# Laying the layers' first projections into the list of the first attention's last batch

## The chip, the cores and the metric

The kernel runs on one core of a Trainium2 chip. The metric is the device time of one execution in microseconds; three executions of the kernel before gave 3595.04 to 3600.91 us, median 3598.8 us.

## The reference, cut to what matters

The input is 8 batches of 512 tokens with 128 features. A block of two parts is applied:

```python
# part 1, "attention": queries, keys of 16 heads x 16 features, values of 64
A = tril((1 + q.k/4 + (q.k)^2/32))          # taylor features of q and k, multiplied out
y = A @ v;  y = y * rsqrt(mean(y*y) + 1e-5) * g;  out = y @ Wo.T
...
# part 2, six layers: x = x + local_attention(x); x = x + feed_forward(x)
qkv = x @ Wqkv                               # 16 heads of 64; q, k scaled to length 1
q, k = rotary(q), rotary(k)                  # two tables and a swap of halves
attn = softmax(q.k * 8 over the own and the previous window of 32) ; x += (attn @ v) @ Wo
x += W2 @ (a * gelu(gate)),  (a, gate) = layernorm(x) @ W1
```

Around both parts stand layer norms over the 128 features ("in" ahead of the attention, "mid" behind it, "x" ahead of the layers, "end" behind them). So the layers of a batch need that batch's attention and two norms, but nothing of another batch.

## The kernel before, in words

All work is cut into stages, each with a short name and a key. The function `order()` makes one list of all stages; each engine's program walks this one list from front to back and issues its own part of every stage that it has a part in. So within an engine the order is the order of the list, and between engines only semaphores count. `order()` gives each stage a place, a number from the table PLACE plus a multiple for its batch, tick or slot, and sorts by it. Places have no direct meaning in time: they fix only who comes ahead of whom.

The attention has 8 batches with 24 ticks each; one tick is a place unit. AS (scores) writes banks 0 to 3 of PSUM in turn, ASa and ASd square and mask them, AY multiplies with the values into bank 4, AE copies the sum to AO, AEa squares it, AR sums the squares into bank 5. AI1 to AI3 form the root of the mean square (logarithm and exponential on ScalarE, then three Newton steps on VectorE and a split), AM spreads it over the partitions, AMd multiplies, AO (8 accumulated products) projects. Then the norms mid and x, each as N1 (product on TensorE, Square and Copy on ScalarE), N2 (mean on TensorE) and N3 (Ln and Exp on ScalarE, three steps on VectorE); between them AZ (a VectorE product and a GpSimd addition); at the end AW writes X, the layers' input. In the steady part the tail of batch b lies beside the ticks of batch b+1; behind batch 7 there is no next batch.

The layers have 384 slots, one for each of 6 layers, 8 batches and 8 pairs of heads; one slot is a place unit there. LW loads a chunk of the weights into one of three buffers WS (issued from ScalarE's queue, and the fourth waits until GpSimd is through with the first), WC rounds it into LH on ScalarE, WL writes the rest into LL on GpSimd. XS and XSl do the same with X. PJ (one for q and one for k of each slot) multiplies three times on TensorE; PQ squares on ScalarE; PT multiplies with the rotary tables on VectorE; TS swaps halves by DMA; AD adds on GpSimd; SS sums squares on TensorE into bank 4. For every four slots NM1, NM2 form the roots, RW writes them to DRAM, RQ turns them for the queries, and RB (one per slot) reads them back, spread over the partitions; PR multiplies K with them on GpSimd. S1 (one per two slots) is the first score product; it needs PR of both slots. MX, S3, SU, NP, TT, PX, PV follow. LO and L2 load the output and feed-forward weights.

What matters here: `order()` calls `run()` behind the attention, which empties its plan, and only then plans the layers. So every layer stage comes behind AW of batch 7 in every engine's queue, and LW 0, LO, L2 and XS wait for `xa_dve` 16 (all of X) besides. The layers' memory overlays the attention's: the inner `ExitStack` is closed ahead of LH. Three banks, 5 to 7, serve the layers' groups in a ring; the attention's own ring is 6 and 7.

Of the kernel before, what the change touches and what calls it, by code (L numbers as in the profile page):

```python
# [138 lines left out]
def order():  # L139
# [21 lines left out]
    def norm(kind, b, z, places):  # L161
# [40 lines left out]
    run()  # L202
    o.ring, o.busy = [5, 6, 7], {}

    def group(st, i, by, value):
        at = o.ring.pop(0)
        o.ring.append(at)
        o.hold(at, st, (i,), 0)  # L210
        o.busy[at] = (by, value)
        o.put(st, i)


    for l in range(DEPTH):
# [11 lines left out]
        at(first + 2, o.put, "L1", l)
        at(first + 4, group, "WB", l, "wb_dve", l + 1)
        at(first + 9, o.put, "W1", l)
        at(first + 9.9, o.put, "W1l", l)  # L230
        at(first + 5 if l else -9.5, o.put, "LO", l)
        at(first + 10 if l else -9.5, o.put, "L2", l)
    for u in range(NB * DEPTH):
        z = 8 * u
# [12 lines left out]
        at(z + P["F3l"], o.put, "F3l", u)
        for i in range(2):
            at(z + P["TB"][i], o.put, "TB", u, i)
        for i in range(3):  # L250
            at(z + P["F4"][i], group, "F4g", 3 * u + i, "f4_act", 3 * u + i + 1)
            at(z + P["F4"][i], group, "F4a", 3 * u + i, "f4_dve", 3 * u + i + 1)
        at(z + P["F5"], group, "F5", u, "f5_dve", 2 * u + 2)
    for n in range(NS):
        for w in range(2):
            i = 2 * n + w
            at(n + P["PJ"][w], group, "PJ", i, "pj_dve", i + 1)
            at(n + P["PQ"][w], o.put, "PQ", i)
            at(n + P["PT"][w], o.put, "PT", i)
            at(n + P["SS"], o.put, "SS", i)  # L260
            at(n + P["AD"], o.put, "AD", i)
        at(n + P["TS"], o.put, "TS", n)
        at(n + P["RB"], o.put, "RB", n)
        at(n + P["PR"], o.put, "PR", n)
        if n % 4 == 0:
            at(n + P["NM1"], o.put, "NM1", n // 4)
            at(n + P["NM2"], o.put, "NM2", n // 4)
            at(n + P["RW"], o.put, "RW", n // 4)
            at(n + P["RQ"], group, "RQ", n // 4, "rq_act", n // 4 + 1)
        if n % 2 == 0:  # L270
            m = n // 2
            for st in ("S1", "MX", "SU", "NP", "TT", "PX", "PVn"):
                at(n + P[st], o.put, st, m)
            for i in range(4):
                at(n + P["S3"][i], o.put, "S3", m, i)
                at(n + P["PV"][i], o.put, "PV", m, i)
    for b in range(NB):
        z = 8 * (NB * (DEPTH - 1) + b)
        at(z + P["E1"], o.put, "E1", b)
        norm("end", b, z, P["EN"])  # L280
        at(z + P["E2"], o.put, "E2", b)
        at(z + P["E3"], o.put, "E3", b, banks=[(None, "e3_act", 1, 1)])
# [4 lines left out]
def build(nc, xin, cst, awq, awk, awv, awo, wqkv, wo, w1, w2, vec, out):  # L287
    o = order()
    no = o.no
    with ExitStack() as ctx:  # L290
# [12 lines left out]
        with ExitStack() as ca:  # L303
            WH = sb("WH", [128, 1536], F32R, ca)
            WL = sb("WL", [128, 1536], F32R, ca)
            WOA = sb("WOA", [128, 8, 128], F32, ca)
            V = sb("VA", [128, 4, 1024], F32, ca)
            AO = [sb(f"AO{i}", [128, 8, L], F32, ca) for i in range(2)]
            bselr = sb("bselr", [128, 1024], F32R, ca)
# [3 lines left out]
            XR = [sb(f"XR{i}", [128, L], F32, ca) for i in range(4)]  # L313
            T = [sb(f"T{i}", [128, L], F32, ca) for i in range(11)]
            SQ = [sb(f"sq{i}", [128, L], F32, ca) for i in range(4)]
            NQ = [sb(f"NQ{i}", [128, L], F32, ca) for i in range(3)]
            NZ = [sb(f"NZ{i}", [128, L], F32, ca) for i in range(3)]
            R = [sb(f"R{i}", [128, L], F32R, ca) for i in range(2)]
# [1061 lines left out]
```

## Time and profile before

| | before |
|---|---|
| median of three executions | 3598.8 us |
| the profiled execution | 3589.28 us, its span 3587.4 us |
| TensorE busy | 3341.0 us, 93% |
| VectorE busy | 2770.1 us, 77% |
| ScalarE busy | 2550.7 us, 71% |
| GpSimd busy | 2031.3 us, 57% |

The span goes from the first to the last instruction. The profile's names: PE is TensorE's products, PEld its weight loads, DVE VectorE, ACT ScalarE, POOL GpSimd, SP SyncE; a "q" behind a name is that engine's queue issuing a DMA. L509 is the line of the helper that issues every product, so products are told apart by the tiles behind them: `PS<-AO,WOA` is AO, `PS<-R,bselr` AM, `PS<-LXH,LH` the first of a PJ's three products (or one of VP's), `PS<-SX,C` SS, `PS<-K,Q` S1. The profiled execution is 9.5 us faster than the median; differences are formed within it and then taken off the median.

### The profile page before, as it was taken

Reading aid. Unit: us, or ns where it says so; the run is one execution under the profiler, and the core shown is the slowest. Engines: PE = TensorE matmul, PEld = TensorE weight load, DVE = VectorE, ACT = ScalarE, POOL = GpSimd, SP = SyncE. Lnnn points to the kernel's source line nnn. Section 1 sums busy time; section 2 is a strip of 40 time slices with the busy share of each in tenths; the row PEclk is TensorE's granted clock in tenths of the full one; section 3 lists DMA queues with packets and bytes.
Section 4 is the critical chain, followed back from the end, with each engine's and each line's share of the span. In section 5 each row is a group of like instructions: output and inputs, shape, how many; then the busy total and the mean of one; then the engine's idle time right before and its main releaser. Section 6 shows DMA issues by size and latency. Waiting matters only on the chain.

```text
span 3587.4 us, 149059 instructions
## 1 busy us (share of the span) xinstructions
PE 3341.0 (93%) x65032; PEld 2107.9 (59%) x65032; DVE 2770.1 (77%) x3420; ACT 2550.7 (71%) x5866; POOL 2031.3 (57%) x1557
## 2 busy tenths in 40 slices
PE   7999995999999999999999999999999999999996
PEld 3444433666666666666666666666666666666663
DVE  3656654888888887888888888888887888788873
ACT  4666563777777777777677777777677777687774
POOL 0000004766677666776666776667676667676661
PEclk9999997999999999999999999999999999999998
DMA  3322322433343333443333333334333333333330
GB/s 100 77 76 75 80 56 89 149 126 126 130 139 132 127 119 126 133 136 128 126 125 131 136 134 123 128 122 142 128 128 126 125 134 128 131 126 129 129 120 24
DMA packets 247337, 423.34 MB, mean 118 GB/s; under 512 B 71966, under 2 KB 110108, under 8 KB 246556
## 3 DMA queue, kind: packets, MB, share of 16 engines
q1 hardware_dynamic: 220368, 397.28, 32.8%
q10 hardware_dynamic: 26316, 16.52, 1.6%
q8 instruction: 511, 8.37, 0.9%
q14 instruction: 142, 1.16, 0.1%
HBM read 124.21 MB, written 7.34 MB: 37 GB/s over the span
## 4 chain that ended last, share of the span: by engine, by line
PE 64%; DVE 16%; issue 7%; POOL 5%; ACT 5%; DMA 2%; SPq 1%; ACTq 0%; DVEq 0%; POOLq 0%
PE PS L509 63%; DVE TPB L904 5%; DVE MX L928 2%; ACT SC L1204 1%; DVE NV L919 1%; POOL K L1291 1%; POOL Q L1309 1%; DMA RB<-root_scratch 1%; POOL K L1309 1%; DVE PP L949 1%; DVE PX L950 1%; DVE NV L917 1%; DVE H L772 1%; ACT SX L1180 1%; SPq L451 1%
## 5 line engine op out<-in xcount | busy, mean ns | idle before, releaser
L904 DVE SCALAR_TENSOR_TENSOR TPB<-PS,VEC,C 128x1024 f32<-128x1024 f32 x768 | 962.1, 1270 | 117.3 <-ACT SX L1180 110.6
L1204 ACT ACTIVATE SC<-PS,BQ,RQ 128x64 f32<-128x64 f32 x3072 | 971.6, 435 | 37.5 <-DVE BQ L933 37.0
L1180 ACT ACTIVATE SX<-PS 128x512 f32<-128x512 f32 x768 | 459.6, 613 | 390.5 <-PE PS L509 387.6
L1291 POOL TENSOR_TENSOR K<-K,RB 128x512 f32<-128x512 f32 x384 | 493.7, 1286 | 280.1 <-DMA RB<-root_scratch 275.9
L1314 POOL TENSOR_TENSOR SC<-SC,RC 128x1024 f32<-128x1024 f32 x192 | 366.1, 1907 | 475.0 <-DVE RC L941 474.9
L509 PEld LDWEIGHTS PS<-PP,VV 32*64 32x64 f32 x24576 | 432.6, 133 | 276.8 <-issue 274.5
L509 PE MATMUL PS<-PP,VV 32*64 32x64 f32 (+1 forms) x24576 | 539.8, 223 | 7.7 <-issue 6.4
L1309 POOL TENSOR_TENSOR K<-TPB,TR 128x512 f32<-128x512 f32 x384 | 496.9, 1294 | 0.0
L1309 POOL TENSOR_TENSOR Q<-TPB,TR 128x512 f32<-128x512 f32 x384 | 495.3, 1290 | 0.0
L509 PE MATMUL PS<-LXH,LH 128*128 128x512 f32 x768 | 369.2, 481 | 89.0 <-DVE TPB L904 62.3
L509 PE MATMUL PS<-K,Q 64*32 64x64 f32 (+1 forms) x24576 | 302.2, 224 | 46.9 <-issue 43.0
L509 PE MATMUL PS<-AOT,LO 128*128 128x512 f32 x768 | 342.7, 599 | 0.0
L509 PEld LDWEIGHTS PS<-K,Q 64*32 64x32 f32 x24576 | 286.8, 105 | 69.7 <-issue 55.5
L939 DVE TENSOR_REDUCE SM<-SC 128x16 f32<-128x1024 f32 x192 | 233.9, 1218 | 108.4 <-ACT SC L1204 106.5
L1194 ACT COPY VV<-PS 128x512 f32<-128x512 f32 x384 | 230.2, 599 | 119.1 <-PE PS L509 118.0
L509 PE MATMUL PS<-LXH,LL 128*128 128x512 f32 x768 | 305.4, 398 | 0.0
L509 PE MATMUL PS<-LXL,LH 128*128 128x512 f32 x768 | 305.0, 397 | 0.3 <-issue 0.3
L928 DVE TENSOR_REDUCE MX<-PS 128x16 f32<-128x1024 f32 x192 | 233.9, 1218 | 46.6 <-PE PS L509 46.0
L509 PEld LDWEIGHTS PS<-LXH,LH 128*128 128x128 f32 x768 | 145.1, 189 | 202.9 <-DVE TPB L904 94.2
L509 PE MATMUL PS<-SX,C 128*32 128x128 f32 x6144 | 254.7, 281 | 8.3 <-issue 4.3
L1257 POOL TENSOR_TENSOR XR<-XR,T 128x512 f32<-128x512 f32 x8 | 11.1, 1389 | 424.2 <-DVE T L874 424.2
L509 PEld LDWEIGHTS PS<-AOT,LO 128*128 128x128 f32 x768 | 142.2, 190 | 170.2 <-issue 169.9
(166 smaller groups left out, 5840.1 us busy)
## 6 DMA issues: line engine op xcount, KB each, us to landing
TR<-TPB SPq DMA_DIRECT2D x768, 256.0 KB, 2.7
RB<-root_scratch SPq DMA_DIRECT2D x768, 128.0 KB, 3.0
PP<-PX SPq DMA_DIRECT2D x192, 192.0 KB, 2.5
WS<-in_wqkv ACTq DMA_DIRECT2D x72, 128.0 KB, 2.5
PP<-PX SPq DMA_DIRECT2D x192, 48.0 KB, 2.3
QA<-TH SPq DMA_DIRECT2D x128, 64.0 KB, 2.1
QA<-TL SPq DMA_DIRECT2D x128, 64.0 KB, 2.1
KA<-TH SPq DMA_DIRECT2D x128, 64.0 KB, 2.1
```

The lines of the kernel that those rows point to most:

```text
L451: e.dma_start((QA, KA)[n][c::4, g % 6, :].bitcast(F32), (TH, TL)[low][rows, n, half, :].bitcast(F32)).then_inc(sem[f"qk_in{g % 2}"], 16)
L509: return e.matmul(dst, lhsT, rhs, start=start, stop=stop, **kw)
L772: e.scalar_tensor_tensor(u, u, -0.5, x, ALU.mult, ALU.mult).then_inc(sem[done], 1)
L904: e.scalar_tensor_tensor(TPB[:, n % 3:4 + n % 2:3 + n % 2 - n % 3, w, :], g, VEC[:, l, 9 + w:10 + w], C[:, at:at + 1024].rearrange("p (o c ...
L928: e.tensor_reduce(MX[:, :], g, AX_X, ALU.max).then_inc(sem["s1_dve"], 1)
L939: e.tensor_reduce(SM[:, :], SC[m % 2][:, :, :, :].rearrange("p g x k -> p g (x k)"), AX_X, ALU.add).then_inc(sem["su_dve"], 1)
L1180: e.activation(SX[i % 3][:, :], bk("PJ", key)[:, :], ACT.Square).then_inc(sem["pj_act"], 1)
L1194: e.copy(VV[:, c, 512 * hf:512 * hf + 512], bk("VP", key)[:, :]).then_inc(sem["vp_act"], 1)
L1204: p = e.activation(SC[m % 2][:, g, :, :].rearrange("p x k -> p (x k)"), bank[s][:, at:at + 64], ACT.Exp, bias=BQ[m % 2][:, g:g + 1], scale ...
L1291: e.tensor_tensor(dst, dst, RB[n % 2][:, :], ALU.mult).then_inc(sem["pr_pool"], 1)
L1309: e.tensor_tensor((Q, K)[w][:, n % 8, :], TPB[:, n % 3, w, :], TR[n % 2][:, w, :], ALU.add).then_inc(sem["ad_pool"], 1)
L1314: e.tensor_tensor(sc, sc, RC[m % 2][:, :].rearrange("p (g o) -> p g o", o=1).broadcast_to([128, 16, 64]), ALU.mult).then_inc(sem["np_pool" ...
```

## The change

The layers' stages go into the same plan as the attention's. A layer place t stands at LS + 2.9 t, with LS 221, in the attention's units; a batch of the attention is 24 units, so batch 7's last tick has place 190.8 (AS) to 191.8 (AY). PJ 0 then stands at 198.9, between AM 2 and AM 3 of batch 7, and S1 0 at 220.8, behind AW of batch 7 (215.1). The main order of TensorE's queue from AR of batch 7 on, worked out from the two formulas (AM, AO of batch 7 with the number of the head pair):

```
AR, AM0, AM1, AM2, AO0, PJ0, AM3, AO1, AO2, AM4, PJ1, AO3, AM5, AO4, AM6, PJ2, AO5, SS0, SS1, AM7, AO6, PJ3, AO7,
N1 mid, PJ4, SS2, SS3, N2 mid, PJ5, PJ6, SS4, SS5, PJ7, PJ8, SS6, SS7, N1 x, N2 x, PJ9, PJ10, SS8, SS9, PJ11,
RQ0, PJ12, SS10, SS11, PJ13, VP0, PJ14, SS12, SS13, PJ15, S1 0
```

VectorE's queue over the same stretch, and ScalarE's and GpSimd's in part:

```
VectorE: AI1, AI2, AI3, AMd0..4, PT0, AMd5, PT1, AMd6, AMd7, PT2, PT3, N3 mid, PT4, PT5, AZ, PT6, PT7, NM1, PT8, NM2, PT9,
         N3 x, PT10, PT11, AW, PT12, PT13, PT14, PT15, MX 0
ScalarE: AEa7, AI1, LW0..2, XS0, AI3, WC0, LW3, WC1, LW4, WC2, LW5, PQ0, PQ1, WC3, LW6, WC4, LW7, PQ2, PQ3, AO7, WC5, LW8, WC6, LW9,
         N1 mid, PQ4, N3 mid, PQ5, WC7, LW10, WC8, LW11, PQ6, PQ7, WC9, WC10, PQ8, N1 x, NM1, PQ9, WC11, N3 x, PQ10, ...
GpSimd:  XSl0, WL0..4, WL5, WL6, AD0, AD1, WL7, WL8, AD2, AD3, AZ, WL9, WL10, AD4, AD5, WL11, AD6, AD7, PR0, AD8, AD9, XSl1, AD10, AD11, PR1
SyncE:   TS0, TS1, TS2, AZ, TS3, RW0, TS4, RB0, TS5, RB1, TS6, RB2
```

LW 0 no longer waits for all of X but for the attention's last use of the memory under LH, LL, WS and their neighbours; XS 0 waits for X of batch 0 alone; LO and L2 keep the wait for all of X and stand at layer place -0.8. The early groups take banks 1 to 3, which AS has left, and from layer place -1.2 on the ring is 5, 6, 7 as before; S1 0 waits until the early groups have left banks 1 to 3. Memory is laid out so that what the layers need first lies under what the attention leaves first, with a gap of 2944 columns. All other places are set anew by small amounts. In the layers' steady part the resulting order is the same on VectorE; on ScalarE XS comes one place earlier, ahead of S3's second quarter instead of behind it, and F4g moves ahead of a few instructions for two batches of a layer; on TensorE S1 comes ahead of WB once in each layer; on GpSimd XSl is one place earlier once in a layer; on SyncE E1 and E3 of the last layer change places with a neighbour. In the attention's steady part some ten neighbours change places on TensorE, and as many on VectorE and ScalarE, in each batch.

```diff
+SLOT = 2.9
...
+    "LS": 221.000, "LB": -1.200, "LO": -0.800, "S1": -0.074, "MX": 0.116, "S3": (0.544, 0.762, 0.998, 1.143),
...
+    "XS": -9.372, "XSl": -9.254, "VP": -0.635, "VC": -0.652, "WO": (12.673, 12.742, 12.742, 12.755),
...
-    run()
-    o.ring, o.busy = [5, 6, 7], {}
...
+    early = [1, 2, 3]
+
+    def lay(t, f, *a, **kw):
+        at(P["LS"] + SLOT * t, f, *a, **kw)
+
+    def begin():
+        for i in early:
+            o.busy[i] = ("as_act", 24 * NB)
+
+    def switch():
+        o.first = [o.busy[i] for i in early]
+        o.ring = [5, 6, 7]
+        o.busy[5] = ("ao_act", NB)
+        early.clear()
+
+    lay(-12, begin)
+    lay(P["LB"], switch)
 
     def group(st, i, by, value):
-        at = o.ring.pop(0)
-        o.ring.append(at)
+        ring = early or o.ring
+        at = ring.pop(0)
+        ring.append(at)
         o.hold(at, st, (i,), 0)
...
-            at(place[0] - 2 if l else -9.5, o.put, "LW", 12 * l + c)
+            lay(place[0] - 2 if l else -9.5, o.put, "LW", 12 * l + c)
...
-        at(first + 5 if l else -9.5, o.put, "LO", l)
-        at(first + 10 if l else -9.5, o.put, "L2", l)
+        lay(first + 5 if l else P["LO"], o.put, "LO", l)
+        lay(first + 10 if l else P["LO"], o.put, "L2", l)
...
+            sb("gap", [128, 2944], F32, ca)
...
         def xready(u):
             l, b = lb(u)
-            return ("f5_dve", 2 * (u - NB) + 2) if l else ("xa_dve", 16)
+            return ("f5_dve", 2 * (u - NB) + 2) if l else ("xa_dve", 2 * b + 2)
...
                 elif st == "S1":
                     m, = key
+                    for name, value in [] if m else o.first:
+                        on.wait_ge(name, value)
...
                     if i == 0:
-                        on.wait_ge("xa_dve", 16)
-                        for b in range(NB):
-                            on.wait_ge(f"x1_out{b}", 16)
+                        on.wait_ge("ay_pe", 24 * NB)
+                        on.wait_ge("ac_pe", NB)
+                        on.wait_ge("av_pe", 8 * NB)
+                        on.wait_ge("ao_pe", NB - 1)
+                        on.wait_ge("ae_dve", 8 * NB)
+                        on.wait_ge("ax_pool", NB)
...
                     l, = key
+                    on.wait_ge("w1_act", l + 1)
                     if l == 0:
                         for z in (W1H, W1L):
                             e.memset(z[:, :, F1:384].bitcast(F32), 0.0)
-                    on.wait_ge("w1_act", l + 1)
```

## Rows read from the trace of the kernel before

**Rows 1.** The page: busy time, and the span in 40 slices of 89.7 us.

```profile
PE 3341.0 (93%) x65032; PEld 2107.9 (59%) x65032; DVE 2770.1 (77%) x3420; ACT 2550.7 (71%) x5866; POOL 2031.3 (57%) x1557
...
PE   7999995999999999999999999999999999999996
...
PEclk9999997999999999999999999999999999999998
```

**Rows 2.** Windows: busy us of PE, PEld, DVE, ACT, POOL (instructions), granted clock, DMA.

```profile
534.80:574.05 39.25, 18.82 (x40) 7.11 (x40) 16.90 (x24) 7.87 (x13) 1.26 (x1) 0.71 0.02 7
574.05:617.66 43.61, 26.33 (x173) 14.79 (x173) 22.01 (x20) 15.53 (x34) 26.10 (x27) 0.75 0.44 150
617.66:650.00 32.34, 28.65 (x660) 19.88 (x664) 26.22 (x33) 22.50 (x66) 28.51 (x22) 0.89 0.45 160
```

**Rows 3.** Timeline of batch 7's tail: start, us, engine, instruction, idle before.

```profile
538.52 0.63 ACT L992 ACTIVATE T<-T 128x512 f32<-128x512 f32 x1
...
542.82 1.22 PE L509 MATMUL PS<-R,bselr 128*128 128x512 f32 x2 [6.24 <-DVE R L781]
...
554.68 0.58 ACT L1160 COPY T<-PS 128x512 f32<-128x512 f32 x1 [12.70 <-PE PS L509]
...
555.31 1.12 PE L509 MATMUL PS<-T,C 128*128 128x512 f32 x2 [0.73 <-ACT T L1160]
...
566.88 2.08 PE L509 MATMUL PS<-NQ,C 128*128 128x512 f32 x2 [0.74 <-ACT NQ L1089]
```

**Rows 4.** Timeline of the layers' start.

```profile
574.05 1.43 ACTq L1022 DMA_DIRECT2D WS<-in_wqkv  x3
...
580.45 0.79 PE L509 MATMUL PS<-LXH,LH 128*128 128x512 f32 x1 [11.50 <-POOL LL L1285]
...
604.45 1.73 SPq L482 DMA_DIRECT2D root_scratch<-NV  x4
...
606.27 1.11 SPq L474 DMA_DIRECT2D TR<-TPB  x2
...
607.43 1.25 SPq L492 DMA_DIRECT2D RB<-root_scratch  x2
...
611.39 1.28 POOL L1291 TENSOR_TENSOR K<-K,RB 128x512 f32<-128x512 f32 x1 [4.62 <-DMA RB<-root_scratch]
...
617.66 1.46 PE L509 MATMUL PS<-K,Q 64*32 64x32 f32 x128 [2.57 <-POOL K L1291]
```

**Rows 5.** Groups of instructions, 574.05 to 617.66: busy us, mean ns of one, idle before.

```profile
L904 DVE SCALAR_TENSOR_TENSOR TPB<-PS,VEC,C 128x1024 f32<-128x1024 f32 x16 | 19.9, 1278 | 21.6 <-ACT SX L1180 19.5 <-POOL K L1309 2.1
L509 PE MATMUL PS<-LXH,LH 128*128 128x512 f32 x16 | 9.5, 594 | 15.1 <-POOL LL L1285 11.5 <-DVE TPB L904 3.6
L1180 ACT ACTIVATE SX<-PS 128x512 f32<-128x512 f32 x16 | 9.1, 595 | 11.1 <-PE PS L509 8.6 <-POOL LL L1285 2.5
L1285 POOL TENSOR_TENSOR LL<-WS,LH 128x256 fp32r<-128x256 f32 x12 | 8.7, 731 | 8.5 <-ACT LH L1056 8.5
L509 PE MATMUL PS<-LXL,LH 128*128 128x512 f32 x16 | 7.9, 496 | 0.0
...
L509 PE MATMUL PS<-SX,C 128*32 128x128 f32 x112 | 5.9, 313 | 3.0 <-ACT SX L1180 2.8
...
L1056 ACT CAST LH<-WS 128x256 fp32r<-128x256 f32 x12 | 4.8, 406 | 7.6 <-POOL LL L1285 7.6
```

**Rows 6.** VectorE's line L772 (second Newton step) by tiles: shortest/median/longest ns.

```profile
L772 DVE SCALAR_TENSOR_TENSOR H<-H,FX x48: 691/1048/1489, 713.1 to 3555.3; 128x512 f32<-128x512 f32 x48
L772 DVE SCALAR_TENSOR_TENSOR NQ<-NQ,NZ x24: 691/692/694, 18.3 to 571.1; 128x512 f32<-128x512 f32 x24
```

**Rows 7.** Waits of TensorE from 100 to 500 us: us in total, times, longest.

```profile
PE PS L509 <- DVE PA L842: 5.1, 7, 0.9
PE PS L509 <- DVE AO L852: 2.2, 6, 1.0
```

**Rows 8.** The line of XS: its instructions, shortest/median/longest ns.

```profile
L1069 ACT CAST LXH<-X x48: 610/669/678, 577.8 to 3399.5; 128x512 fp32r<-128x512 f32 x48
```

More of the change, by code:

```diff
@@ L227, in order @@
[L227 to L230, printed above, removed]
-        at(first + 5 if l else -9.5, o.put, "LO", l)
-        at(first + 10 if l else -9.5, o.put, "L2", l)
+                lay(place[c] + 2 * (l > 0), o.put, "LW", 12 * l + c + 3)
+        lay(first + 2, o.put, "L1", l)
+        lay(first + 4, group, "WB", l, "wb_dve", l + 1)
+        lay(first + 9, o.put, "W1", l)
+        lay(first + 9.9, o.put, "W1l", l)
@@ L256, in order @@
             i = 2 * n + w
[L257 to L264, printed above, removed]
+            lay(n + P["PJ"][w], group, "PJ", i, "pj_dve", i + 1)
+            lay(n + P["PQ"][w], o.put, "PQ", i)
+            lay(n + P["PT"][w], o.put, "PT", i)
+            lay(n + P["SS"], o.put, "SS", i)
+            lay(n + P["AD"], o.put, "AD", i)
+        lay(n + P["TS"], o.put, "TS", n)
+        lay(n + P["RB"], o.put, "RB", n)
+        lay(n + P["PR"], o.put, "PR", n)
         if n % 4 == 0:
[L266 to L269, printed above, removed]
+            lay(n + P["NM1"], o.put, "NM1", n // 4)
+            lay(n + P["NM2"], o.put, "NM2", n // 4)
+            lay(n + P["RW"], o.put, "RW", n // 4)
+            lay(n + P["RQ"], group, "RQ", n // 4, "rq_act", n // 4 + 1)
         if n % 2 == 0:
@@ L272, in order @@
             for st in ("S1", "MX", "SU", "NP", "TT", "PX", "PVn"):
-                at(n + P[st], o.put, st, m)
+                lay(n + P[st], o.put, st, m)
             for i in range(4):
-                at(n + P["S3"][i], o.put, "S3", m, i)
-                at(n + P["PV"][i], o.put, "PV", m, i)
+                lay(n + P["S3"][i], o.put, "S3", m, i)
+                lay(n + P["PV"][i], o.put, "PV", m, i)
     for b in range(NB):
         z = 8 * (NB * (DEPTH - 1) + b)
[L279 to L282, printed above, removed]
+        lay(z + P["E1"], o.put, "E1", b)
+        norm("end", b, z, P["EN"], lay)
+        lay(z + P["E2"], o.put, "E2", b)
+        lay(z + P["E3"], o.put, "E3", b, banks=[(None, "e3_act", 1, 1)])
     run()
@@ L305, in build @@
             WL = sb("WL", [128, 1536], F32R, ca)
-            WOA = sb("WOA", [128, 8, 128], F32, ca)
             V = sb("VA", [128, 4, 1024], F32, ca)
-            AO = [sb(f"AO{i}", [128, 8, L], F32, ca) for i in range(2)]
-            bselr = sb("bselr", [128, 1024], F32R, ca)
+            AO0 = sb("AO0", [128, 8, L], F32, ca)
             cumt = [sb(f"cumt{i}", [128, 32], F32, ca) for i in range(2)]
@@ L312, in build @@
             CX = [sb(f"CX{i}", [128, 8], F32R, ca) for i in range(2)]
[L313 to L318, printed above, removed]
+            XIN, XNC = (sb(n, [128, L], F32, ca) for n in ("XIN", "XNC"))
+            NQ = [sb("NQ0", [128, L], F32, ca)]
+            NZ = [sb("NZ0", [128, L], F32, ca)]
             XP = [(sb(f"XH{i}", [128, L], F32R, ca), sb(f"XL{i}", [128, L], F32R, ca)) for i in range(2)]
@@ L356, in build @@
         RB = [sb(f"RB{i}", [128, L]) for i in range(2)]
+        VV = sb("VV", [128, 4, 1024])
+        LO = sb("LO", [128, 8, 128])
+        W1H = sb("W1H", [128, 2, 384], F32R)
+        W1L = sb("W1L", [128, 2, 384], F32R)
+        W2 = sb("W2", [128, 3, 128])
+        AOT = sb("AOT", [128, 8, L])
+        EU = sb("EU", [128, L])
+        ER = sb("ER", [128, L])
+        EX = sb("EX", [128, L])
+        ES = sb("ES", [128, L])
+        EZ = sb("EZ", [128, L])
+        SC = [sb(f"SC{i}", [128, 16, 2, 32]) for i in range(2)]
+        PP = [sb(f"PP{i}", [128, 2, 16, 32]) for i in range(2)]
+        PX = sb("PX", [128, 16, 32])
         XCH = sb("XCH", [128, L], F32R)
@@ L1031, in scalar_program @@
                     else:
-                        on.wait_ge("xa_dve", 16)
+                        on.wait_ge("xa_dve", 2 * NB)
+                        for b in range(NB):
+                            on.wait_ge(f"x1_out{b}", 16)
                     e.dma_start(LO[:, :, :], wo[l].rearrange("(c p) d -> p c d", p=128)).then_inc(sem["wo_in"], 16)
```

60 lines of the change are left out of this document (27 added, 33 removed), and 23 rows, old and new, of the table PLACE.

## The prediction, made blind

> **What bounds the kernel now.** I read the page first: TensorE is busy for 93% of the span, and the slices show where it is not: at the start, at the end, and in the seventh slice, 538 to 628 us, where its digit falls to 5 and the granted clock to 7 [rows 1]. The reader should see there one hole in an otherwise full engine. The windows split the hole. From 534.80 (batch 7's last AE is being written) to 574.05 (its AW ends) TensorE is busy 18.82 of 39.25 us, VectorE 16.90, ScalarE 7.87, GpSimd 1.26. From 574.05 to 617.66 (S1 0) TensorE is busy 26.33 of 43.61 us, VectorE 22.01, ScalarE 15.53, GpSimd 26.10; the clock is 0.71 and 0.75, so between the two levels of 1.2 and 2.4 GHz and mostly near the lower [rows 2]. Both stretches are chains in which one engine waits for the next: the timeline shows TensorE idle for 6.24 us ahead of AM 0, ScalarE for 12.70 ahead of the copy behind AO 7, and TensorE for 11.50 ahead of PJ 0 [rows 3, 4]. The second chain needs nothing of the first but memory and the queues' order, as X of batch 0 is complete seven batches earlier. Behind S1 0 TensorE is busy 28.65 of 32.34 us [rows 2] and soon full. So the time follows S1 0: if it comes g us earlier and the order behind it is the old one, the end comes g us earlier.
>
> **When the layers can start.** LW 0 to 2 now stand in ScalarE's queue behind AI1 of batch 7. Its exponential ends at 538.52 + 0.63 = 539.15 [rows 3]; the memory's last user, AE, is done at 534.8 [rows 2]. So LW 0 is issued at 539.2 and not at 574.05 [rows 4], 34.9 us earlier. If nothing of the tail stood in the way, S1 0 would come at 539.2 + 43.61 = 582.8. That is the upper end of the gain, 34.9 us. VectorE's work of both stretches, 16.90 + 22.01 = 38.9 us from 534.8 on, and TensorE's, 45.15, would fit into it.
>
> **What the mixing costs the tail.** In a queue in order, what is put between two tail stages delays them unless the tail was waiting anyway. I go down the orders of the front part. Prices: a PJ is 0.594 + two at 0.496 = 1.59 us; an SS 5.9 / 14 = 0.42 (112 products are 14 SS); PQ 0.60; PT 1.28; WC 0.41; WL 0.73 [rows 5]; one LW issue 1.43 / 3 = 0.48 [rows 4].
> 1. AM 0 to AO 7 (542.82 to 554.68, [rows 3]): TensorE gets four PJ and two SS more, 4 x 1.59 + 2 x 0.42 = +7.2 us. Its gaps there are short, so I count all of it. Two PT stand among the AMd, but each AMd has its AM a place ahead; hidden under TensorE.
> 2. ScalarE's part of N1 mid stands behind WC 5, LW 8, WC 6, LW 9, and LW 8 and 9 wait for WL 5 and 6: 0.41 + 0.73 + 0.48 + 0.41 + 0.73 + 0.48 = 3.2 us, beside the 1.12 us of N1's product [rows 3]: +2.0.
> 3. PJ 4, SS 2 and 3 ahead of N2 mid, 2.4 us, lie beside N1's Square and Copy, which point 2 has already made late: 0.
> 4. AZ on VectorE stands behind PT 4 and 5, 2 x 1.28: +2.5; on GpSimd behind WL 8 and AD 2 and 3, mostly done before: +1.0 (0 to 2.5).
> 5. N3 x stands behind PT 9 on VectorE, which needs PQ 9, which needs PJ 9, which stands behind N2 x: 1.59 + 0.60 + 1.28 = 3.5, beside the Ln and Exp of N3, twice some 0.65 us (an Exp took 0.63 [rows 3]): +2.0.
> 6. AW stands behind PT 10 and 11: +2.5.
> 7. The products of N1 x and N2 x took 2.08 us each at the low clock; in a busier TensorE I take the 1.12 us that the same of "mid" took [rows 3]: -1.9, if the clock rises.
>
> Sum: 7.2 + 2.0 + 3.5 + 2.0 + 2.5 - 1.9 = 15.3 us.
>
> **GpSimd beside VectorE.** This has to be priced too. The Newton step L772 takes 691 to 694 ns all through the attention, where GpSimd is nearly idle, and 1048 in the median in the layers, where it is at work [rows 6]. The new order puts seven such steps of the tail (two in each N3, one AZ, two AW) beside GpSimd's 26 us of work. At the median's excess of 0.36 us that is +2.5, with every one at the longest 5.6, with none beside a GpSimd instruction 0; I take +2.0, as GpSimd is not at work all the time. The tail then takes 17.3 us more, and AW ends at 574.0 + 17.3 = 591.3.
>
> The Trainium skill has a rule on this that speaks against the change ("GPSIMD Engine Reference", section Specifications): GpSimd shares its SBUF interfaces with VectorE, and VectorE instructions with two SBUF inputs contend with it. L772 reads two tiles in SBUF, and its two lengths agree with it. By that rule the sum is the one above with +2.0, without it 2.0 us better.
>
> **From there to S1 0.** S1 0 needs PR 0 and PR 1. Before, RW was issued at 604.45, RB 0 at 607.43 and PR 0 began at 611.39 [rows 4]. NM2 now ends near 582, ahead of PT 9; TS 4 waits for PT 9 (584), so RB 0 goes near 585 and lands 4.0 us later, at 589. RB 1 is the late one: in SyncE's queue TS 5 stands ahead of it and waits for PT 11, the instruction ahead of AW, at 591.3 - 1.4 = 589.9. TS takes 1.11 us, RB 1.25 [rows 4], landing as above some 2.5 behind the second issue: 594.8. PR 1 takes 1.28 [rows 4]: S1 0 at 596.1. PJ 12 to 15, XS 1 and AD 8 to 11 lie beside this. Gain: 617.66 - 596.1 = 21.5 us.
>
> **The rest.** New waits of S1 0 on banks 1 to 3: they were left many stages ago, 0. LO and L2 are still issued from ScalarE, now ahead of VC 0 instead of ahead of XS 0, with four issues; their data is wanted 13 slots later, 0 to 2 us. Weights or memory at other addresses, banks 5 to 7 in another turn: nothing in the trace hangs on which. The attention's steady part: TensorE waits 7.3 us in 400 us there [rows 7], so new neighbours can win 10 us (over all 520) at the very most if all waits went, and every loss must be an added wait; I take 0 with +-3. The layers: VectorE's order is unchanged; XS ahead of S3's second quarter delays that quarter alone by 0.67 us [rows 8], since the third stood behind XS before too; S1 waits for all four, so 0. Start and end of the kernel: one or two swaps, +-1.
>
> Sum: -21.5 us. Profiled, 3589.28 becomes about 3568 (span 3566); against the median of the runs, 3598.8 - 21.5 = **3577**.
>
> **The rivals.**
> - *The layers' start runs almost untouched* (the planner's interleaving falls into the tail's waits, the clock rises at once): gain 28 to 34.9 us, at 31 a time of 3568. For it: VectorE and TensorE have 40 us of idle time in the two stretches together. Against it: points 1 and 6 stand in the queues whatever the clock. 0.18.
> - *The tail stretches further*, since each of some thirty crossings between engines is a chance to wait and the low clock stays: the 17.3 us become 27, gain 12 us, 3587. For it: the clock of 0.71 and 0.75 [rows 2]; point 7 falls away, PJ at 1.9 us instead of 1.59 add over 2 us more, and two GpSimd instructions per seven steps another 3.6. 0.20.
> - *The change doesn't bring what it does* because the start of the layers is paid back: an S1 0 that is early finds TensorE, VectorE or the RB round trip not ready and the first slots run slower than before; gain below 7.2 us, about 3595. Against it: TensorE has 3.7 us of idle time in the 32 us behind S1 0 [rows 2], little to show such a chain. 0.09.
> - *Slower*: XS. 48 of them stand one quarter of S3 earlier, 0.67 us each. If that quarter's lateness reached TensorE each time, it would cost 48 x 0.669 = 32.1 us against 21.5: 3609. It decides from 32 of 48 on. For it: S3 releases SU and the next S1. Against it: the end of all four quarters does not move. 0.05.
>
> **How the numbers follow.** The forecast (gain 15 to 28, 3571 to 3584) has 0.48. What a measurement of this kernel can tell from no change is 0.2%, 7.2 us. Faster by more: 0.48 + 0.18 + 0.20 = 0.86, less a little for the joint error of the steady parts (+-4) at the edge: 0.85. The rest: same 0.10, slower 0.05. The range for 8 in 10 takes in the two neighbours: gain 34.9 to 9 less the spread of some us, 3565 to 3591.
>
> **What would show it.** In the changed kernel's profile LW 0 should be issued near 539 and not 574, the copy behind AO 7 near 562, AW end near 591, S1 0 start near 596. The seventh slice's TensorE digit should be 7 or 8. L772 on NQ should have a longest value over 1 us. TensorE's waits from 100 to 500 us should stay near 7.3. The distance from S1 0 to the end should be the old 3587.4 - 617.7 = 2969.7 us. I am wrong if S1 0 is later than 608 (the tail is what stretches), or if this last distance changes by more than 5 us (then it is the small moves of places, not the overlap, that carry the result).

## The result and the profile after

Before and after together on one chip: 3599.86 us (median of 4) and 3555.52 us (median of 4), ratio 0.988 with the 95% interval 0.9859 to 0.9901. The changed kernel is faster, as forecast, but by 44 us and not by 21, and its time lies 9.5 us under the range. On a second chip (e14 below) the ratio was 0.9866 (0.984 to 0.9891).

The page of the changed kernel answers to [rows 1]. The seventh slice now covers 533 to 622 us.

```profile
PE 3325.9 (94%) x65032; PEld 2107.6 (59%) x65032; DVE 2737.3 (77%) x3420; ACT 2545.5 (72%) x5866; POOL 2041.5 (57%) x1557
...
PE   7999987999999999999999999999999999999996
...
PEclk9999998999999999999999999999999999999998
```

The digit of the seventh slice rose from 5 to 7, its clock from 7 to 8. The profiled execution took 3555.15 us, its span 3553.3.

Windows answer to [rows 2]: from AI1 of batch 7 to the end of its AO 7, from there to S1 0, both together from 3.2 us earlier on (the place in the work where 534.80 stands in [rows 2]), and from S1 0 to the end. Each row gives the length, then busy us and instructions of TensorE, its weight loads, VectorE, ScalarE and GpSimd, then the granted clock and the DMA.

```profile
522.63:544.07 21.44, 15.02 (x52) 8.08 (x52) 13.20 (x17) 6.70 (x13) 5.74 (x6) 0.74 0.25 74
544.07:578.12 34.05, 23.28 (x154) 12.88 (x161) 24.24 (x24) 14.75 (x32) 23.96 (x22) 0.80 0.37 129
...
519.40:578.12 58.72, 40.24 (x214) 21.16 (x221) 38.80 (x43) 22.08 (x46) 29.71 (x28) 0.77 0.30 102
...
578.12:3553.30 2975.18, 2797.43 (x62468) 1867.50 (x62452) 2401.07 (x2852) 2200.60 (x5335) 1992.32 (x1508) 0.99 0.37 126
```

The third of these rows holds the same work as both stretches of 82.9 us in [rows 2]: VectorE's 38.80 us of work now lie in 58.72 us, where they were spread over 82.9. The timeline of the stretch, to be laid beside [rows 3] and [rows 4]:

```profile
524.16 1.43 ACTq L1053 DMA_DIRECT2D WS<-in_wqkv  x3
...
528.63 1.22 PE L535 MATMUL PS<-R,bselr 128*128 128x512 f32 x2 [6.48 <-DVE R L809]
...
544.15 0.59 ACT L1193 COPY T<-PS 128x512 f32<-128x512 f32 x1 [0.26 <-PE PS L535]
...
556.02 1.78 DVE L902 TENSOR_TENSOR T<-T,NZ 128x512 f32<-128x512 f32 x1
...
559.22 2.07 PE L535 MATMUL PS<-XR,C 128*128 128x512 f32 x2 [0.32 <-POOL XR L1290]
...
564.01 1.73 SPq L508 DMA_DIRECT2D root_scratch<-NV  x4
...
566.85 1.80 DVE L800 SCALAR_TENSOR_TENSOR NQ<-NQ,NZ 128x512 f32<-128x512 f32 x1
...
572.59 1.66 DVE L910 TENSOR_TENSOR X<-T,NZ 64x512 f32<-64x512 f32 x1
...
576.62 1.29 POOL L1324 TENSOR_TENSOR K<-K,RB 128x512 f32<-128x512 f32 x1
...
578.12 1.53 PE L535 MATMUL PS<-K,Q 64*32 64x32 f32 x124
```

The reader should take two differences from this timeline. AM 0 of batch 7 starts at 528.63 where it started at 542.82 [rows 3]: 14.2 us were won *before* the layers' first product (LW 0, the first layer stage, goes out at 524.16). And from AM 0 to S1 0 it is 49.5 us where it was 74.8: 25.3 us more. S1 0 comes 39.5 us earlier. Behind S1 0 the layers take 2975.2 us where they took 2969.7.

The row of AI3's last step (first and last start of 8 batches) shows where the 14 us come from, before and after:

```profile
L781 DVE SCALAR_TENSOR_TENSOR R<-T,C x8: 740/742/752, 109.9 to 542.0; 128x512 fp32r<-128x512 f32 x8
```

```profile
L809 DVE SCALAR_TENSOR_TENSOR R<-T,C x8: 741/751/999, 105.8 to 527.6; 128x512 fp32r<-128x512 f32 x8
```

4.1 us are there by batch 0. Windows from one such step to the next (batches 1 to 2 and 2 to 3), first before, then after:

```profile
172.50:235.02 62.52, 61.40 (x300) 26.90 (x299) 39.17 (x70) 40.78 (x63) 2.68 (x2) 0.99 0.30 77
235.02:299.03 64.01, 62.89 (x304) 27.95 (x303) 39.15 (x69) 40.97 (x63) 2.68 (x2) 0.98 0.28 75
```

```profile
167.36:229.00 61.64, 61.10 (x302) 27.10 (x300) 38.59 (x68) 40.68 (x63) 2.55 (x2) 1.00 0.30 78
229.00:290.61 61.61, 61.07 (x302) 27.09 (x300) 38.58 (x68) 40.72 (x63) 2.55 (x2) 1.00 0.30 78
```

A batch took 62.5 or 64.0 us, and now 61.6. TensorE's idle time fell from 1.12 to 0.54 us per batch, and the granted clock went from 0.99 or 0.98 to 1.00: the same products cost less. Between batch 5 and 6 the distance fell from 61.5 to 58.5 us. The stretch ahead of batch 0's AI3, before and after:

```profile
0.00:109.91 109.91, 82.06 (x370) 40.72 (x371) 43.96 (x84) 53.91 (x81) 4.18 (x10) 0.92 0.34 98
```

```profile
0.00:105.78 105.78, 83.38 (x379) 42.23 (x379) 44.73 (x84) 54.47 (x83) 4.19 (x10) 0.92 0.36 102
```

Here TensorE's idle time fell from 27.9 to 22.4 us. Added up to AI3 of batch 7, TensorE was idle for 45.2 us before and 37.4 after, and busy for 496.8 and 490.2 us (these are sums of such rows over all eight batches) with the same products. So 7.8 of the 14.4 us are idle time and 6.6 are products that took less time at the higher clock.

These two parts do not rest equally firmly. The idle time comes out alike in other executions (44.7 us in e15, the kernel before again; 37.8 in e16 and 39.5 in e1, which have the changed kernel's order of the attention). The clock does not. In e16 three batches show 0.97, one of them:

```profile
230.88:294.02 63.14, 62.77 (x304) 27.56 (x300) 38.69 (x69) 40.72 (x63) 2.55 (x2) 0.97 0.29 76
```

Of the batches 1 to 5, those that took over a microsecond longer than the shortest ones were 14 of 25 in the five profiles with the attention of before (before, e2, e3, e8, e15) and 8 of 30 in the six with the changed one (changed, e1, e4, e12, e14, e16). AI3 of batch 7 stands at 539.9 to 543.5 in the five and at 526.4 to 531.0 in the six, so the gain there is 14.0 us by the means, and a single profile is good for some 2 us either way.

### The profile page after: what moved, and what is told of

Its sections match the earlier page's. It is cut to its first block, busy times and chain, and to the rows that moved or that the text cites. A ratio compares the mean times of both kernels' runs of the same rounds, so it can differ in the third digit from the quotient of the medians.

```text
span 3553.3 us, 149054 instructions
## 1 busy us (share of the span) xinstructions
PE 3325.9 (94%) x65032; PEld 2107.6 (59%) x65032; DVE 2737.3 (77%) x3420; ACT 2545.5 (72%) x5866; POOL 2041.5 (57%) x1557
## 4 chain that ended last, share of the span: by engine, by line
PE 64%; DVE 17%; issue 7%; ACT 5%; POOL 5%; DMA 1%; SPq 1%; DVEq 0%; POOLq 0%; ACTq 0%
PE PS L535 64%; DVE TPB L932 5%; DVE MX L956 2%; ACT SC L1237 1%; DVE NV L947 1%; POOL K L1324 1%; POOL Q L1342 1%; DMA RB<-root_scratch 1%; POOL K L1342 1%; DVE PP L977 1%; DVE PX L978 1%; DVE NV L945 1%; DVE H L800 1%; DVE H L1000 1%; DVE NV L949 1%
## 5 line engine op out<-in xcount | busy, mean ns | idle before, releaser
L535 PE MATMUL PS<-K,Q 64*32 64x64 f32 (+1 forms) x24576 | 302.2, 224 | 49.5 <-issue 48.0
```

The lines of the kernel that those rows point to most:

```text
L535: return e.matmul(dst, lhsT, rhs, start=start, stop=stop, **kw)
```

## The experiments

All times below are of profiled executions unless a ratio is named; "MX 0" is the first row reduction behind S1 0, which VectorE starts 1.5 to 3.4 us behind it. e5 to e9 were executed once each, so they have no ratio, and only their times inside the profile are used.

| kernel | ratio to before (95%) | AI3 of batch 0, 7 | MX 0 | span |
|---|---|---|---|---|
| before | | 109.9, 542.0 | 619.2 | 3587.4 |
| changed | 0.988 (0.9859-0.9901) | 105.8, 527.6 | 581.4 | 3553.3 |
| e1 attention's places alone | 0.9963 (0.995-0.9975) | 104.3, 526.4 | 603.7 | 3574.8 |
| e2 changed, attention's places of before | 0.9932 (0.9914-0.9951) | 108.6, 543.5 | 598.6 | 3576.2 |
| e3 layers' places alone | 0.9988 (0.9973-1.0003) | 107.8, 539.9 | 616.6 | 3581.9 |
| e4 changed, layers late (LS 247) | 0.9933 (0.9916-0.9951) | 103.9, 528.4 | 600.6 | 3567.9 |
| e5 NX, ASd alone | one execution | 109.5, 547.6 | 624.8 | 3597.3 |
| e6 AL, NI, AX, AXp, AC, ACd alone | one execution | 102.8, 532.6 | 609.5 | 3581.2 |
| e7 AR, AI, AM, AMd, AO alone | one execution | 113.2, 541.7 | 619.2 | 3587.3 |
| e8 LO, L2 late alone | one execution | 108.7, 540.8 | 616.0 | 3586.3 |
| e9 e6 and e7 together | one execution | 103.5, 527.0 | 605.1 | 3577.3 |
| e10 changed, norms' steps in PSUM | 0.9887 (0.9858-0.9916) | 102.9, 532.0 | 583.7 | 3562.5 |
| e12 changed, LS 225 | 0.99 (0.9873-0.9927) | 103.0, 527.6 | 595.6 | 3556.5 |
| e14 changed again | 0.9866 (0.984-0.9891) | 105.0, 526.7 | 580.0 | 3552.7 |
| e15 before again | 0.9994 (0.9981-1.0007) | 110.2, 543.4 | 620.2 | 3605.9 |
| e16 changed, AZ of batch 7 earlier | 0.9877 (0.9857-0.9898) | 105.1, 531.0 | 587.3 | 3553.2 |
| e17 e16 and batch 7's norms in PSUM | 0.9878 (0.9859-0.9897) | 104.7, 527.7 | 582.8 | 3545.9 |

**e1: the attention's places without the overlap.** The kernel before, with the 27 attention entries of PLACE from the change.

```diff
-    "F5": 17.001, "E1": 17.594, ..., "AL": -34.770, "NI": (-33.699, -31.527, -30.022), "AX": -28.135, ...
+    "F5": 17.001, "E1": 17.594, ..., "AL": -36.012, "NI": (-34.527, -31.629, -30.525), "AX": -28.436, ...
```

> The kernel before with the attention's 27 entries of PLACE taken from the changed kernel, nothing else. Theory A (the new order within the attention is what the prediction missed): batch 7's AI3 ends 14 us earlier, near 528 instead of 542.8, the stretch from there to S1 0 keeps its 75 us, and the time falls by 13 to 15 us. Rival (the attention's gain comes with the other memory layout or the merged list): AI3 of batch 7 stays near 542 and the time within 3 us of before.

AI3 of batch 7 at 526.4 (-15.7), AM 0 (527.2) to S1 0 (602.1) 74.9 us as before; the ratio is 13.3 us. Theory A holds, the rival falls: neither memory nor the merged list is needed for it.

**e2: the overlap without them.** The opposite edit, in the changed kernel.

```diff
-    ... "AL": -36.012, "NI": (-34.527, -31.629, -30.525), "AX": -28.436, ...
+    ... "AL": -34.770, "NI": (-33.699, -31.527, -30.022), "AX": -28.135, ...
```

> The changed kernel with the attention's entries of PLACE put back to those of before; the overlap, banks, memory and layers' places stay. Theory A: AI3 of batch 7 ends near 542 again, AM 0 to S1 0 takes about 50 us (before 75, changed 49.5), and the time is 25 us under before. Rival: it keeps the whole 39 us at S1 0, since the order within the attention costs nothing.

AI3 of batch 7 at 543.5, AM 0 (544.5) to S1 0 (596.3) 51.8 us, ratio 0.9932, so 24.4 us. The two halves are separate. Their sum is 13.3 + 24.4 = 37.7 us by the ratios, with about 8 us either way by the two intervals (the changed kernel's ratio gives 43.2), and 15.6 + 27.2 = 42.8 by the medians, against 44.3 by the medians for the changed kernel. So they add up as far as can be told.

**e3: the layers' places alone.**

```diff
-    "S1": 0.054, "MX": 0.146, "S3": (0.569, 0.787, 0.863, 1.168), ... "XS": -9.172, "XSl": -9.099,
+    "S1": -0.074, "MX": 0.116, "S3": (0.544, 0.762, 0.998, 1.143), ... "XS": -9.372, "XSl": -9.254,
```

> The kernel before with only the layers' entries of PLACE from the changed kernel (XS one quarter of S3 earlier, F4g and S1 past a weight stage). The prediction: 0, within 3 us, as VectorE's order is the same and the other moves stand beside waits. Rival 1: it explains the 5 us by which the medians differ more (44) than the start of S1 0 (39.5), so 5 us faster. Rival 2 (the prediction's slower case): up to 32 us slower.

The ratio 0.9988 has an interval that holds 1: 4 us faster at the middle, between 10 faster and 1 slower. Rival 2, the 32 us of XS, is excluded. Whether these places give some us or none stays open.

**e4: the layers late.**

```diff
-    "LS": 221.000,
+    "LS": 247.000,
```

> The changed kernel with LS at 247 instead of 221: the layers' first stage then comes behind AW of batch 7 again, all else is the changed kernel's (order within the attention, banks, memory). Overlap theory: S1 0 falls back by 25 us relative to AI3 of batch 7 (AM 0 to S1 0 near 75 us), and the time is 25 us over the changed kernel, 14 under before. Rival (banks 1 to 3 or the memory bring it): it stays within 5 us of the changed kernel.

24.1 us under before where 14 were expected: AM 0 (529.2) to S1 0 (598.8) takes 69.6 us and not 75. So 5 of the changed kernel's 25 us at S1 0 do not need the layers' products beside the tail. The timeline of e4 and the next experiment tell where they come from:

```profile
556.61 1.43 ACTq L1053 DMA_DIRECT2D WS<-in_wqkv  x3
...
559.43 1.56 DVE L909 TENSOR_TENSOR X<-T,NZ 64x512 f32<-64x512 f32 x1
```

LW 0 no longer waits for AW of batch 7, and goes out 28.2 us behind AI3 instead of 32.0 (542.01 to 574.05). That is 3.8 us, and the loads LO and L2 behind the first projections are 1.9 more (e8); together 5.7 for the 5.3 seen. That the banks or the memory layout give nothing of it was not tested by itself.

**e8: the four loads behind the first projections.**

```diff
-        at(first + 5 if l else -9.5, o.put, "LO", l)
-        at(first + 10 if l else -9.5, o.put, "L2", l)
+        at(first + 5 if l else -0.8, o.put, "LO", l)
+        at(first + 10 if l else -0.8, o.put, "L2", l)
```

> The kernel before with the loads LO and L2 at layer place -0.8 instead of -9.5, nothing else: four DMA issues, 2.25 us in ScalarE's queue, no longer stand between LW and XS 0. The kernel with the layers late (LS 247) needed 72.2 us from AI3 of batch 7 to MX 0 where before needed 77.2. Theory: 2 us of these 5 are this move, so 75 us here. Rival: the move costs ahead of VC 0 what it saves ahead of XS 0: 77 us.

AI3 to MX 0 took 75.3 us (before 77.2): 1.9 us, the theory's number. The eight profiles whose joint is that of before (before, e1, e3, e5, e6, e7, e9, e15) lie between 76.7 and 78.2, so the sign is clear and the size is good for about 1 us. The prediction had this edit at 0 to 2 us of *loss*.

**e5, e6, e7, e9: which of the attention's places.** Each is the kernel before with some entries of PLACE from the change; e9 has those of e6 and of e7.

```diff
+    e5: "NX": (43.175, 43.864, 44.884), "ASd": -1.145
+    e6: "AL": -36.012, "NI": (-34.527, -31.629, -30.525), "AX": -28.436, "AXp": -24.593, "AC": -22.471, "ACd": -23.232
+    e7: "AR": (13.810, 25.331), "AI": (24.704, 25.305, 26.769), "AM": (28.659, 0.832), "AMd": -0.684, "AO": (30.495, 0.702)
```

> The kernel before with two of the attention's entries from the changed kernel: NX (the x norm's places, N3 later) and ASd (the mask, earlier). It takes the mask of tick 94 ahead of the three VectorE steps of batch 2's x norm, and the same in every batch. Theory A1 (that one swap is the 0.9 us per batch by which the period of the attention's batches fell, 62.5 to 61.6): the period falls to 61.6 and AI3 of batch 7 comes 5 to 6 us earlier, 536 to 537. Rival (the many small swaps share it): below 2 us, AI3 of batch 7 above 540.

> The kernel before with AL, NI, AX, AXp, AC, ACd (load, in norm, running sums of a coming batch) from the changed kernel. Theory A2 (these earlier stages are the 4 us by which batch 0's AI3 came earlier, and nothing later): AI3 of batch 0 at 106 instead of 109.9, the later period as before at 62.5, AI3 of batch 7 at 538. Rival: batch 0 unchanged at 109.9.

> The kernel before with AR, AI, AM, AMd, AO (a batch's own tail beside the next batch's ticks) from the changed kernel. Theory A3: they carry what is left of the 14 us, 3 us between the AI3 of batches 6 and 7's neighbours (58.5 instead of 61.5 for batch 6) and the moments at the low clock that come 6 us behind an AI3. Rival: nothing, since TensorE is full there, AI3 of batch 7 at 542.

> The kernel before with the entries of both earlier subsets: AL, NI, AX, AXp, AC, ACd and AR, AI, AM, AMd, AO. Alone they moved AI3 of batch 7 by -9.4 and -0.3 us, and all 27 entries by -15.7. Theory (the gain comes of these two together): within 3 us of 526.4. Rival (the entries left, AQ, AV, AS, AE, NM, AZ, NX, AW, are needed for the period of 61.6): the period stays over 62.3 and AI3 of batch 7 over 531.

e5 contradicts theory A1: it is later, not earlier, by 5.6 us at AI3 of batch 7, with 63.1 to 64.6 us per batch. e6 wins 7.1 us by batch 0 and 9.4 by batch 7, with its batches at 62.9 to 63.4 us; e7 loses 3.3 by batch 0 and is level by batch 7, at 62.7 to 63.4. Neither subset reaches 61.6. Both together do in three of five batches (the other two took 62.9 and 63.4 us at a clock of 0.97), and e9's AI3 of batch 7 is at 527.0, within 0.6 us of e1. One of the three:

```profile
165.03:226.63 61.60, 61.12 (x301) 27.00 (x301) 38.59 (x70) 40.96 (x62) 2.67 (x2) 1.00 0.30 78
```

So 11 of the 27 entries carry the 15 us. Alone the two subsets give -9.4 and -0.3, in one kernel -15.0. Each of these is one execution, and executions of one order differ by 4 us at this point, so the 5 us beyond the sum are likely but not shown. TensorE's idle time, which repeats better, says the same for the steady part: it was 1.12 us per batch before, 0.6 to 1.5 in e6 (1.12 in the mean), 1.0 to 1.1 in e7, and 0.5 in every batch of e9. Which neighbour of which decides was not taken further.

**e10, e17: the steps beside GpSimd.** In e10 every norm's three steps keep their intermediate in the norm's own bank, and the bank is given back behind the third step; in e17 batch 7's alone, on top of e16.

```diff
-                    rsqrt(bk("N2", key)[:, :], nsq(kind)[:, :], nroot(kind)[:, :], kind + "_log", kind + "_root", b)
+                    rsqrt(bk("N2", key)[:, :], bk("N2", key)[:, :], nroot(kind)[:, :], kind + "_log", kind + "_root", b)
...
-        o.keep(o.bank["N2", (kind, b), 0], kind + "_root", 3 * b + 1)
+        o.keep(o.bank["N2", (kind, b), 0], kind + "_root", 3 * b + 3)
```

> The changed kernel; in the norms' three VectorE steps the intermediate goes to the norm's own PSUM bank instead of an SBUF tile, so that steps 2 and 3 read one SBUF tile and not two (the bank is given back two steps later). Theory (contention with GpSimd lengthened these steps in the mixed stretch: step 2 took 1.80 us beside GpSimd, 0.69 without): both go to 0.65 to 0.70 us in each norm, S1 0 comes 1 to 2 us earlier, the time moves by less than can be told. Rival (their length there is a wait for something else): step 2 of batch 7's x norm still takes over 1 us.

The second step by tiles, e10 (to be laid beside the 1.80 us of the changed kernel's timeline):

```profile
L800 DVE SCALAR_TENSOR_TENSOR PS<-PS,NZ x24: 699/700/700, 18.6 to 570.7; 128x512 f32<-128x512 f32 x24
```

The longest fell from 1.80 to 0.70 us, although in e10 too an addition on GpSimd (570.65 to 571.92) ran through all of this step of batch 7's x norm (570.67 to 571.37). So the length was contention with GpSimd over SBUF. The edit moves the step's output to PSUM together with one of its two inputs; the step ahead of it in the changed kernel, which reads PSUM and one SBUF tile and writes to SBUF, took 0.69 us beside GpSimd (566.13), which points at the second input. But AM 0 to S1 0 took 48.8 us instead of 49.5, 0.6 us, AZ still took 1.73 us, and the attention lost 4.5 us (AI3 of batch 7 at 532.0). TensorE now waits for the bank. The waits of TensorE from 100 to 500 us in e10:

```profile
PE PS L535 <- DVE NZ L802: 3.4, 5, 0.7
PE PS L535 <- DVE PA L870: 2.4, 7, 0.4
```

The first line is new: the changed kernel has only the other two kinds (3.3 us, see below). In the time e10 is slower than the changed kernel beside it by 9 us of medians (3558.86 and 3549.83). A bank released 1.4 us later in every norm costs more here than a step that is 1.1 us longer in one.

**e12: the start of the layers four places later.**

```diff
-    "LS": 221.000,
+    "LS": 225.000,
```

> The changed kernel with LS at 225 instead of 221: the layers' start stands 4 places later, PJ 0 behind AO 6 of batch 7 instead of behind AO 0, PT 0 behind the last AMd, AW ahead of PT 10 and 11. Theory (S1 0 hangs on the layers' own chain, and the tail has slack): AW of batch 7 ends 4 to 8 us earlier, but S1 0 comes 3 to 7 us later. Rival (the tail is what S1 0 waits for, as the prediction's sum had it): S1 0 comes earlier with it.

AW ends at 576.5, 2.3 us *later* than in the changed kernel, and S1 0 comes at 593.9, 65.5 us behind AM 0 instead of 49.5. Both numbers of the theory miss; its direction, S1 0 hanging on the layers' own chain, holds more strongly than it said. The waits from 528 to 594 us in e12 name the place:

```profile
POOL LL L1318 <- ACT LH L1089: 23.1, 8, 11.1
...
ACT LH L1089 <- POOL LL L1318: 12.5, 5, 6.3
```

GpSimd's WL waits 23.1 us for ScalarE's WC (18.8 in the changed kernel), once 11.1: the fourth WC stands in ScalarE's queue behind PQ 0 and PQ 1, which wait for PJ 0 and PJ 1, which now stand behind AO 6, and here behind the copy of AO 7 and N1 of the norm mid as well. In the time the loss is smaller, 0.99 against 0.9866 on the same chip (11 us by the medians, 3560.86 and 3549.83).

**e16, e17: AZ of batch 7 ahead of the layer work.**

```diff
-        at(z + P["AZ"], o.put, "AZ", b)
+        at(z + P["AZ"] - 2.06 * (b == NB - 1), o.put, "AZ", b)
```

> The changed kernel with one stage moved: AZ of batch 7 stands 2.06 places earlier, right behind N3 of the norm mid and so ahead of PT 4 and 5 on VectorE and of WL 7, WL 8, AD 2 and AD 3 on GpSimd. Theory (head-of-line blocking of the tail by layer work is what stretches it): N1 of the x norm starts 3 to 4 us earlier, S1 0 comes 2 to 3 us earlier, the time falls by about 2 us. Rival (S1 0 hangs on the layers' own chain of PT, PJ and PQ): S1 0 moves by less than 1 us.

> As e16_az_early, and the norms of batch 7 alone keep their intermediate in PSUM (steps 2 and 3 read one SBUF tile), so that the attention's steady part is untouched. Theory: batch 0 to 6 as in the changed kernel (AI3 of batch 7 near 527), steps 2 and 3 at 0.69 us each, S1 0 another 1 to 2 us earlier, the best of all kernels here by 3 to 5 us in the trace. Rival: the bank held longer delays PJ or AM as it did in every batch when all norms did it (AI3 of batch 7 at 532).

AZ's product starts 24.6 us behind AM 0 instead of 27.4, but the x norm's first product starts 31.2 us behind it instead of 30.6, as the timeline of e16 shows:

```profile
562.12 1.14 PE L535 MATMUL PS<-SX,C 128*32 128x128 f32 x16 [0.60 <-ACT SX L1213]
...
563.20 2.08 PE L535 MATMUL PS<-XR,C 128*128 128x512 f32 x2
```

It has no wait of its own: it stands in TensorE's queue behind PJ 7, PJ 8, SS 6 and 7, and PJ 7 had waited 3.26 us for a PT, SS 6 0.60 us for its PQ. The other half of the delay is on GpSimd, where the move put AZ's addition ahead of WL 7:

```profile
557.43 1.26 POOL L1290 TENSOR_TENSOR XR<-XR,T 128x512 f32<-128x512 f32 x1 [4.25 <-DVE T L902]
```

GpSimd stood idle for 4.25 us ahead of it, WL 7 began 26.6 us behind AM 0 instead of 23.4, and ScalarE's next WC waited 4.64 us for it. AM 0 to S1 0 took 51.9 us in e16 and 50.9 in e17, against 49.5 and 49.3 in the two profiles of the changed kernel: S1 0 came about 2 us later, which neither the theory nor the rival of e16 had. Both ratios are the changed kernel's within their intervals. In e17 the steps took 0.70 us and AI3 of batch 7 stood at 527.7, so the attention was left alone as meant, and S1 0 came 1.0 us earlier than in e16, though not earlier than in the changed kernel. So the norm's steps are worth 0.6 to 1.0 us at S1 0, by single profiles. AW's 1.66 us stayed in both kernels, and no run took it away.

**e14, e15: the two kernels once more.**

> The changed kernel itself once more, beside the same runs of before as the two below. If the first profile is typical, AI3 of batch 7 starts within 2 us of 527.6, AM 0 to S1 0 takes 49 to 51 us, and the ratio to before is 0.988 to 0.990.

> The kernel before, submitted as if it were a change. What is still open is why the medians differ by 44 to 50 us while the two profiled executions differ by 34. Theory (the profiled execution of before was one with a high granted clock; the executions scatter with the clock): this profile has more time at the low clock than the first and a span nearer 3598, S1 0 between 617 and 621, ratio 1.000 within 0.3%. Rival (the difference sits in a fixed place behind S1 0): S1 0 to the end is 2969.7 us within 2 us again.

e14: AM 0 (527.8) to S1 0 (577.1) 49.3 us. e15: S1 0 at 618.6, and from there to the end 2987.3 us instead of 2969.7, with a mean granted clock of 0.978 instead of 0.981. The windows from S1 0 to the end, first profile of before, then e15:

```profile
617.66:3587.40 2969.74, 2800.13 (x62460) 1866.52 (x62460) 2430.65 (x2851) 2203.46 (x5332) 1983.50 (x1508) 0.99 0.37 126
```

```profile
618.62:3605.90 2987.28, 2807.50 (x62460) 1872.96 (x62460) 2426.76 (x2851) 2204.36 (x5332) 1983.07 (x1508) 0.99 0.37 126
```

The same instructions in the same order differ by 17.5 us between two executions, TensorE's busy time by 7.4. The first profile of before lies 10 us under the median of its own executions, so the 34 us between the first two profiles hold 10 us of luck of the kernel before, and the scatter behind S1 0 is larger than the 5.5 us by which the changed kernel's layers seemed slower. That rival (a fixed place behind S1 0) falls.

## Why the prediction was right or wrong

**The step that failed** is "The attention's steady part: TensorE waits 7.3 us in 400 us there [rows 7], so new neighbours can win 10 us (over all 520) at the very most ...; I take 0 with +-3". It was -14 us (e1: 13.3 by the ratio, 15.7 at AI3 of batch 7). Its bound was wrong in three ways. First, it counted only waits. They did fall, from 7.3 to 3.3 us over the same 400 us in the changed kernel:

```profile
PE PS L535 <- DVE PA L870: 2.3, 7, 0.4
PE PS L535 <- DVE AO L880: 1.0, 1, 1.0
```

But TensorE's busy time fell too, by 6.6 us up to AI3 of batch 7, as the granted clock was 1.00 in batches that had shown 0.98 or 0.99. Second, it looked at 100 to 500 us alone: ahead of batch 0's AI3 TensorE lost 5.4 us of idle time (4.1 us in the time), where the text had "+-1" for the start. Third, it took a row's waits as what an order can be worth and gave the middle as 0, with nothing in the trace that said the old order was as good as the new. By place the parts are 4.1 (start) + 3.0 (batch 6) + 3.0 (two batches at the lower clock) + 4.6 (five batches at 0.9) - 0.3 (batch 7) = 14.4 us. The 3.0 of two batches and about half of batch 6's 3.0 are what single executions differ by: e15 has 60.0 us where before has 61.5, and four batches at 64 where before has two. Why a stretch at the lower clock comes in one batch and not in the next stays open.

**The overlap was right in mechanism** and a little small: AM 0 to S1 0 was forecast at 53.3 us and measured at 49.5, a gain of 25.3 for 21.5.
- Start: LW 0 at 539.2, that is 2.8 us ahead of AI3's last step; measured 3.4 ahead (524.16 and 527.57). Right.
- Point 1 (AM 0 to the copy behind AO 7, +7.2): +3.7 (15.5 us for 11.9). "Its gaps there are short, so I count all of it" was wrong; TensorE had been waiting for VectorE in the gaps, and the work went into them.
- Points 2 to 7 with the contention, 10.1 us together behind AO 7: +10.8 (from the copy to AW's end 30.1 us for 19.3). Right as a sum; its single terms were not taken apart by a run, so part of this may be luck. Inside it the clock did half of what point 7 took: N1 x still cost 2.07 us, N2 x fell to 1.12. (The text put the clocks 0.71 and 0.75 "mostly near the lower" level; 0.75 is halfway between the two.)
- Contention (+2.0): AZ 1.78, the x norm's second step 1.80, AW 1.66, each about 1.1 us over [rows 6]'s 0.69, so 3 to 4 us of lengthening on VectorE. The Trainium skill's rule ("GPSIMD Engine Reference", Specifications: shared SBUF interfaces, contention with two-input VectorE instructions) agrees with e10, where one SBUF input less brought 1.80 back to 0.70. What it costs at S1 0 is known for the norm's step alone, 0.6 us in e10 and 1.0 between e16 and e17; for AZ and AW it stays open. So the +2.0 is neither confirmed nor refuted.
- From AW to S1 0: 4.8 forecast, 3.9 measured (574.25 to 578.12). Right; RB 1 came behind TS 5 behind PT 11 as worked out (TS at 571.84, RB at 573.01).
- LO and L2: "0 to 2 us", as a cost, was the wrong sign, they gave 1.9 us (e8). In the sum against the old S1 0 the four issues ahead of XS 0 had been part of the 43.6 us.

**The rivals.** "Almost untouched" (28 to 34.9 us) came close to the total but not by its mechanism: the overlap gave 25. "Stretches further" did not happen. "Paid back behind S1 0" did not happen as far as can be seen: from MX 0 to the end it is 2961 to 2979 us in the eight profiles with the merged list (mean 2970) and 2965 to 2986 in the nine with the old one (mean 2972). By the prediction's own sign, a change of the last distance by more than 5 us, its 5.5 us pointed to the places; they did carry a third, but the sign was no test, as one kernel differs by 17.5 us there. "Slower by XS" is excluded by e3.

**The range** was right for the overlap (15 to 28) and failed on the independent term: e2, which has the overlap without the attention's places, took 3567.15 us in the median (0.9932 of 3598.8 is 3574), inside 3565 to 3591.

## What to carry to other kernels

When a change resets every place of a hand-made order, price the reordering as a term of its own, with its own range, and test it alone: here it was a third of the gain, was carried by 11 of 27 numbers, and its parts alone did not seem to add up to it. The idle time that this trace showed on the busiest engine was not an upper bound for what an order can win, because the busy time fell as well (6.6 of 14.4 us, with a higher granted clock). When two chains are laid into one list, the late one hangs on its own slowest hand-over (here weights: load, round, rest, and the queue places between), so start that chain first (four places later cost 16 us at the joint). Moving the other chain's blocked step ahead won nothing here (e16, e17), because it made the weights' chain wait on GpSimd.

## What the runs showed that I had not expected

- A batch's period went from 62.5 or 64.0 to 61.6 us while the granted clock went from 0.99 or 0.98 to 1.00, and TensorE's idle time per batch fell by only 0.6 us. In e16, with the same order of the attention, three batches showed 0.97 again and took 62.8 to 63.1 us.
- Two sets of places that each leave the batches at 62.7 to 63.4 us give 61.6 in three of five batches together (e6, e7, e9).
- VectorE instructions with two SBUF inputs beside a working GpSimd took 1.66 to 1.80 us instead of 0.69, with one input and the output in PSUM 0.70 (e10).
- Two executions of one kernel differed by 17.5 us behind S1 0 with mean clocks of 0.981 and 0.978. Differences of two single profiles can't settle 10 us here; the medians and the milestones ahead of the scatter can.
